# Pair products and their PSUM tiles: two column tiles become four tiles of 64 partitions

## The reference, cut to what matters

```python
e = jnp.stack([tbl_0[ids[:, 0]], ..., tbl_25[ids[:, 25]]], axis=1)      # (512, 26, 32)
x1 = jnp.einsum('bik,bjk,hij->bhk', e, e, W1) + b1[None, :, None]       # W1 (128, 26, 26)
x2 = jnp.einsum('bik,bjk,hij->bhk', x1, e, W2) + b2[None, :, None]      # W2 (128, 128, 26)
z = jnp.sum(jnp.concatenate([x1, x2], axis=1), axis=-1)                 # (512, 256)
h = jnp.concatenate([z, dense_ctx], axis=1)                             # 256 + 16
h = jnp.maximum(h @ W_top1 + b_top1, 0.0)                               # 512
h = jnp.maximum(h @ W_top2 + b_top2, 0.0)                               # 256
y = h @ W_top3
```

## Time and profile before

| what | value |
|---|---|
| median of 3 runs (lowest to highest) | 164.78 us (164.68 to 164.88) |
| the profiled execution: its own time | 163.22 us |
| its span, from first to last instruction | 161.4 us |
| busy: PE / PE weight loads / DVE / ACT / POOL | 133.6 / 118.2 / 106.7 / 70.6 / 93.5 us |
| mean granted TensorE clock over the span | 0.968 |

### The profile page before, as it was taken

One profiled execution on the slowest core, in us unless ns is written; L12 is line 12 of the kernel. 1 busy time (PEld: TensorE's weight loads), 2 busy tenths in 40 slices (PEclk: granted clock), 3 DMA queues, 4 the chain that ended last, 5 costly groups with the idle time before them and its releaser, 6 DMA issues.

```text
span 161.4 us, 4180 instructions
## 1 busy us (share of the span) xinstructions
PE 133.6 (83%) x1670; PEld 118.2 (73%) x1670; DVE 106.7 (66%) x413; ACT 70.6 (44%) x189; POOL 93.5 (58%) x100
## 2 busy tenths in 40 slices
PE   6437999910299668998999999799999979999994
PEld 6324666700299557987887899698789968999993
DVE  7889568973999999999106998950699993000000
ACT  1121788943336764041553810255381025683042
POOL 3778777787778777777777777777774000000000
PEclk9999999996559999999999999999999999999999
DMA  6995331000000403001010421000043000032000
GB/s 131 387 304 167 128 113 21 14 8 14 16 15 16 73 15 80 13 12 16 13 19 12 82 72 25 13 12 16 15 81 73 10 0 0 4 60 63 13 0 1
DMA packets 8539, 8.59 MB, mean 53 GB/s; under 512 B 3128, under 2 KB 7650, under 8 KB 8340
## 3 DMA queue, kind: packets, MB, share of 16 engines
q1 hardware_dynamic: 2668, 4.70, 8.9%
q10 hardware_dynamic: 2908, 2.12, 5.9%
q0 software_dynamic: 2944, 1.51, 5.9%
HBM read 7.28 MB, written 1.04 MB: 52 GB/s over the span
## 4 chain that ended last, share of the span: by engine, by line
PE 60%; POOL 17%; issue 6%; DVE 6%; ACT 6%; DMA 3%; ACTq 0%; SPq 0%
POOL emb L321 17%; PE z2p L673 15%; PE ring L636 13%; PE z2p L678 7%; PE ring L642 5%; PE h2y L729 5%; PE ring L657 3%; DVE emb L482 3%; PE ring L666 2%; PE h1p L720 2%; ACT v_in L810 2%; DVE ctx_x L478 2%; PE h1p L721 2%; DMA idx<-in_ids 1%; DMA emb<-in_tbl,idx 1%
## 5 line engine op out<-in xcount | busy, mean ns | idle before, releaser
L321 POOL DMA_INDIRECT emb<-in_tbl,idx x92 | 92.6, 1007 | 29.4 <-issue 27.7
L636 PE MATMUL ring<-r,l 128*64 128x104 f32 x256 | 27.4, 268 | 10.3 <-DVE l L519 10.3
L636 PEld LDWEIGHTS ring<-r,l 128*64 128x64 f32 x256 | 25.2, 147 | 13.0 <-DVE l L519 10.7
L637 PE MATMUL ring<-r,l 128*64 128x104 f32 x256 | 27.4, 268 | 0.0
L637 PEld LDWEIGHTS ring<-r,l 128*64 128x64 f32 x256 | 25.2, 147 | 0.0
L673 PE MATMUL z2p<-t_in,v_in 128*128 128x128 f32 x208 | 24.5, 277 | 0.8 <-ACT v_in L810 0.8
L673 PEld LDWEIGHTS z2p<-t_in,v_in 128*128 128x128 f32 x208 | 23.6, 192 | 1.2 <-ACT v_in L810 1.0
L835 ACT COPY t_in<-ring 128x416 f32<-128x416 f32 x32 | 16.2, 507 | 17.4 <-PE ring L637 17.4
L605 PE MATMUL ring<-w1s,w2t 128*128 128x352 f32 x52 | 17.5, 502 | 3.7 <-DVE w1s L375 3.7
L605 PEld LDWEIGHTS ring<-w1s,w2t 128*128 128x128 f32 x52 | 10.8, 210 | 10.0 <-DVE w1s L375 3.8
L519 DVE TENSOR_TENSOR l<-sg_a,l 128x192 f32<-128x192 f32 (+5 forms) x72 | 15.9, 301 | 0.1
(11 more groups left out here) (138 smaller groups left out, 208.2 us busy)
## 6 DMA issues: line engine op xcount, KB each, us to landing
w2t<-in_L_rec_W SPq DMA_DIRECT2D x1, 1664.0 KB, 7.5
emb<-in_tbl,idx POOLq DMA_INDIRECT x92, 2.4
wt<-in_W_top SPq DMA_DIRECT2D x2, 512.0 KB, 8.6
octet<-in_octet_ids SPq DMA_DIRECT2D x1, 750.0 KB
gram_scratch<-t_in ACTq DMA_DIRECT2D x4, 169.0 KB
gram<-gram_scratch ACTq DMA_DIRECT2D x4, 126.0 KB
small_tbl<-in_tbl SPq DMA_DIRECT2D x4, 125.0 KB
w<-in_L_rec_W SPq DMA_DIRECT2D x1, 338.0 KB, 7.9
```

The lines of the kernel that those rows point to most:

```text
L321: pool.indirect_dma_start(out=emb[:, g, f * K:(f + 1) * K], out_offset=None, in_=a[f"tbl_{f}"][:, :], in_offset=bass.IndirectOffsetOnAxis( ...
L636: pe.matmul(ps[0:HALF, s], l[:, t, 0:HALF], fields, start=True, stop=True)
L637: last = pe.matmul(ps[HALF:P, s], l[:, t, HALF:P], fields, start=True, stop=True)
```

## The change

1. **Tiles of 64 partitions.** A matmul on the block diagonal `R` is cut into its upper and lower 64 rows. A tile t has four matmuls instead of two: two halves h of the rows by two column tiles. Each has 64 rows, 64 (inner) or 42 (across) columns of weights, and half as many moving columns as before, 52 or 26, since a half of the rows holds two of the four samples. The two halves write to two banks. A call of `t_block` makes two blocks (`T_AT` is every second n), with 8 tiles (inner) or 16 (across) to a pair of banks. The blocks stay 8 and 4, and so do the copies and their elements; the copies write their samples two by two.
2. **A ring of four banks.** `z2p` moves into the last quarter of the bank `h2y`, and its bank joins the ring. Layer 3 of the last group writes to `sg_b`. `look_up` of the next group stands after blocks 3 and 5.
3. **Gram transfers on SP.** The five DMAs of each group are issued by SP. SP no longer passes on the gathers: DVE waits for `gathered` itself.
4. **Dummy products.** After `look_up(1)`, PE makes 38 products of `ident` with itself (`WARM_T`) ahead of the first cubes.
5. **Order on DVE.** The two picks for group 1 move from behind `own_terms(1)` into and ahead of `build_b(0)`. In groups 1 and 2 the across products of the first half go behind the fill of R, and the inner cubes wait for two steps of `pairs` there instead of three (`A_WHOLE`).
6. **SBUF.** The inputs of `wt1c` are loaded into `t_in`, which saves two tiles.

```diff
-BLK = 4
-NB = NT // BLK
-XBLK = 8
-TB = NB + NT // XBLK
+BLK = 8
+ROWS = 64
+NB = 2 * (NT // BLK)
+XBLK = 16
+TB = NB + 2 * (NT // XBLK)
-OH_AT = (4, 6)
-WARM_CTX, WARM_VA = 9, 7
-RING = 3
+OH_AT = (3, 5)
+WARM_CTX, WARM_T = 9, 38
+RING = 4
+A_WHOLE = (0, 3)
+T_AT = tuple(range(0, TB, 2))
...
-        zp = [None, ctx.enter_context(nc.psum_tensor("z2p", [P, 512], F32))[:, 0:P]]
-        h2p, yp = [h2y[:, m, :] for m in range(M2)], h2y[0:1, M2, :]
+        h2p, yp, z2p = [h2y[:, m, :] for m in range(M2)], h2y[0:1, M2, :], h2y[:, M2 + 1, :]
...
             for g in range(G):
-                for c, (f0, f1) in enumerate(PARTS):
-                    sp.wait_ge(gathered[g][c], 16 * rows_of(g, f0, f1))
-                    sp.sem_inc(part_in, 1)
+                sp.wait_ge(t_out, TB * g + NB)
+                sp.dma_start(gram_dram[0:NH * NF, :].rearrange("(u v) b -> u v b", v=NF),
+                             t_in[SGL:SGL + NH, :, :]).then_inc(gram_a_stored, 16)
...
@@ take_part
-                dve.wait_ge(part_in, 3 * g + part + 1)
+                dve.wait_ge(gathered[g][part], 16 * rows_of(g, f0, f1))
@@ build_a
-                products(0, across).then_inc(pairs, 1)
+                if g in A_WHOLE:
+                    products(0, across).then_inc(pairs, 1)
@@ build_b
                 fill_r(g, 1)
+                if g == 0:
+                    pick(1, 1)
                 take_part(g, 2)
...
                 fill_r(g, 2)
+                if g not in A_WHOLE:
+                    products(0, across).then_inc(pairs, 1)
                 products(1, across).then_inc(pairs, 1)
@@ t_block
                 if n < NB:
+                    pe.wait_ge(*bank_free("t", TB * g + n + 1))
+                    banks = [ps, bank_of("t", TB * g + n + 1)]
                     for i in range(BLK):
-                        t = n * BLK + i
-                        fields = R[:, t, :, :].rearrange("p q f -> p (q f)")
-                        s = slice(i * 4 * NF, (i + 1) * 4 * NF)
-                        pe.matmul(ps[0:HALF, s], l[:, t, 0:HALF], fields, start=True, stop=True)
-                        last = pe.matmul(ps[HALF:P, s], l[:, t, HALF:P], fields, start=True, stop=True)
+                        t = n // 2 * BLK + i
+                        s = slice(i * 2 * NF, (i + 1) * 2 * NF)
+                        for h in range(2):
+                            r = slice(h * ROWS, (h + 1) * ROWS)
+                            fields = R[r, t, 2 * h:2 * h + 2, :].rearrange("p q f -> p (q f)")
+                            pe.matmul(banks[h][0:HALF, s], l[r, t, 0:HALF], fields, start=True, stop=True)
+                            last = pe.matmul(banks[h][HALF:P, s], l[r, t, HALF:P], fields, start=True, stop=True)
...
+            keep_warm(WARM_T, bank_of("t", 3), bank_free("t", 3))
-            for n in range(TB):
+            for n in T_AT:
                 t_block(0, n, True)
```

More of the change, by code:

```diff
@@ L467, in one_hot, with pick @@
                 dve.wait_ge(octet_step, 4)
-            def pick(g):
+            def pick(g, only=None):
                 for kind, n in picks(g):
                     k = n % 2
+                    if only not in (None, k):
+                        continue
                     dve.wait_ge(picked, n + 1)
@@ L565, in _ @@
             add_unmixed(0)
+            pick(1, 0)
             build_b(0)
@@ L570, in _ @@
             own_terms(1)
-            pick(1)
             for g in range(1, G):
@@ L578, in _, with keep_warm @@
         def _(pe):
-            def keep_warm(count):
+            def keep_warm(count, bank, free=None):
+                if free:
+                    pe.wait_ge(*free)
                 for _ in range(count):
-                    pe.matmul(h1p[:, 0, :], ident[:, :], ident[:, :], start=True, stop=True)
+                    pe.matmul(bank[:, 0:P], ident[:, :], ident[:, :], start=True, stop=True)
             def prepare(n):
@@ new lines, in t_block @@
+                    return
+                pe.wait_ge(*bank_free("t", TB * g + n + 1))
+                banks = [ps, bank_of("t", TB * g + n + 1)]
+                for i in range(XBLK):
+                    t = (n - NB) // 2 * XBLK + i
+                    s = slice(i * 2 * NH, (i + 1) * 2 * NH)
+                    for h in range(2):
+                        r, q = slice(h * ROWS, (h + 1) * ROWS), slice(2 * h, 2 * h + 2)
+                        pe.matmul(banks[h][0:NX, s], l[r, t, P:P + NX], R[r, t, q, NH:NF], start=True, stop=True)
+                        last = pe.matmul(banks[h][HALF:HALF + NX, s], l[r, t, P + NX:LW], R[r, t, q, 0:NH], start=True, stop=True)
+                        if i == XBLK - 1:
+                            last.then_inc(t_done, 1)
@@ L672, in inner @@
                     for j in range(j0, j1):
-                        last = pe.matmul(zp[1], v_in[:, j, :], t_in[:, j, :], start=(start and j == j0), stop=(stop and j == j1 - 1))
+                        last = pe.matmul(z2p, v_in[:, j, :], t_in[:, j, :], start=(start and j == j0), stop=(stop and j == j1 - 1))
                     return last
@@ L677, in across @@
                     for j in range(NH):
-                        last = pe.matmul(zp[1], v_ac[0:MC, j, :], t_ac[0:MC, j, :], start=(start and j == 0), stop=(stop and j == NH - 1))
+                        last = pe.matmul(z2p, v_ac[0:MC, j, :], t_ac[0:MC, j, :], start=(start and j == 0), stop=(stop and j == NH - 1))
                     return last
@@ L767, in _ @@
             layer2(G - 2, h2p)
-            for n in range(TB):
+            for n in T_AT:
                 t_block(G - 1, n, False)
-                if n == L3_AT:
+                if n + 1 == L3_AT:
                     layer3(G - 2, yp)
```

73 lines of the change are left out of this document (29 added, 44 removed).

## The result

The change makes the kernel slower: 183.91 us (182.47 to 186.01, 4 runs) against 164.75 (164.68 to 164.88, 4 runs) on the same chip, a ratio of 1.113 (95% interval 1.107 to 1.120). The forecast was 157.3. The profiled execution took 183.91 for a span of 182.1, 20.7 more than the span before. Two of the warnings that the prediction set out are there: the clock dips after 45 us, and PE is the last to arrive at group 3.

A forecast was written before the change was run, and what follows sets the result against it. PE was taken to bound the kernel, with POOL's gathers and DVE close behind. Group 3 starting 5.4 us earlier plus 2.1 in its cubes gave 7.5 off 164.78: 157.3 us, range 155.0 to 162.0.

The forecast's parts named there:

- Two of the warnings: Signs of a wrong forecast: a clock dip after 45 us; PE still the last to arrive ahead of group 3.
- the price of a pass over a whole stage: Cut cubes on PE: passes of 58 and 39 ns, 6.2 us a group instead of 8.6, down 2.4.
- Rival A: Four tiles not side by side, or PE's issue too slow: 11.5 to 12.5 us a group, 174.7 us; chance 0.12.
- Rival D: The clock falls elsewhere: one spell at 0.50 costs up to 5 us of PE's work, 162.3 us; chance 0.07.
- The dummies: PE's pause before group 0's cubes: 76 passes, 8.7 us from 33.0 to 41.7, hold the clock and cost nothing.
- Group 0: Cubes start at 43.85, sums at 55.8 instead of 59.22, 3.4 us off; group 1's cubes start at 75.7.
- The ring and the copies: ACT's copies bound a cube stage: sums start 2.1 us sooner in group 3, 2.6 in groups 1 and 2.
- The gathers: Group 2's second part lands at 95.1; gathers hold group 3's start to 129.7 instead of 135.12, 5.4 us off.
- rival C: The gathers still land late: group 3 starts at 131.1, time 158.7 us; chance 0.17.
- SP: SP issues the gram's DMAs at no cost; ACT's 1.67 us issue goes, part of group 0's 3.4 us.

The follow-up runs named there:

- mixed: picks_late with the inner cubes of groups 1 and 2 alone cut into four tiles; 159.02 us, ratio 0.976 to the kernel before.
- ring3: pairs_all with a ring of three banks instead of four; 162.95 us, ratio 0.997 to the kernel before.
- a_whole: pairs_all with the first half's across products ahead of the second part in all four groups, as before the change; 159.84 us, ratio 0.981.
- gram_act: pairs_all with the gram's DMAs back on ACT's queue; 159.79 us, ratio 0.977 to the kernel before.
- across_split: pairs_all with each across matmul issued as two with half the moving columns, still 128 rows; 171.22 us, ratio 1.058 to the kernel before.
- pairs_all: The changed kernel without the cut, both kinds of cubes in pairs of 128 rows; 159.07 us, ratio 0.982 to the kernel before.
- no_dummies: pairs_all without the 38 dummy products; 160.51 us, 1.4 more than pairs_all.
- inner_quads: pairs_all with only the inner cubes cut into four tiles; 159.45 us, ratio 0.979 to the kernel before.
- picks_late: pairs_all with group 1's two picks behind the matrices of the second half, and 42 dummies; 158.84 us, ratio 0.981 to the kernel before.

## Why the prediction was wrong, and where it was right

**The step that failed is the price of a pass over a whole stage**: "With 2 ns between passes, as now, I take 58 and 39 ns: 64 x (58 + 39) = 6.2 us a group, down 2.4." Both lengths are right (59 and 41). But a group's cubes are now 1,024 instructions, and these would have to come at 6.1 ns each; over a stage they come at 13.1 [group 3 after: 13.50 us for 1,033]. The rows ahead of the prediction held no row on supply. A row of the page before had it:

```profile
q8 instruction: 13, 0.21, 0.5%
```

These are 13 pieces for 3,340 instructions of PE. Group 3's cubes ran at 522 instructions in 9.51 us, 18.2 ns each, with holes small enough to be taken for nothing. The 4 instructions in 45 ns that I read as a rate were a burst out of what had already been fetched.

The Trainium skill ("Runtime: NRT & Kernel Launch", Instruction fetch mechanics) says that instructions are refilled in blocks of 16 KiB, 256 of them, and that the fetch is hidden because instructions are issued more slowly than they come in. The size of the block agrees with every run here, where the pieces are PE's instructions over 256 to within one. That it is hidden does not: with four tiles PE starts a matmul with its load every 10 to 15 ns, a block is used up in 1.3 to 1.9 us, and the next one takes 3.4 to 4.2.

**Rival A** had the right size for half a reason. It named two ways to a longer pass, tiles that take turns, or PE's instructions "issued no faster than" a rate. The first is shown false: four tiles start within 20 ns. The second is what happened, but as blocks and not as a rate between neighbouring matmuls, and so it bears on the stage and not on the pass. Its formula, 121.2 + 4C, with C = 13.0 (15.70 less 2.7 for look-ups and layer 3) gives a span of 173.2; of the other 8.9 of the 182.1 the rests' clock takes 8.6. The chance of 0.12 was far too low, and the point from which it decides, C = 10.1, was right in kind: 13.0 lies well beyond it. The Trainium skill's 25 ns between starts ("TensorE: Matmul & The Clock Gate", Back-to-back issue gap), weighed there, does not hold across tiles here: starts are 10.2 ns apart. That it would have given a stage of nearly the measured length is a coincidence.

**Rival D**, the clock, was priced for a single spell caused by PE's waits for DVE, with the evidence of small holes that had left the clock at 1.00. What brought it down were the across cubes in four tiles, surely in groups 1 to 3 (a fall near 60 us comes in mixed, ring3 and a_whole as well, whose across cubes are not cut), and once, as it seems, the pause behind the dummies (the same fall comes in gram_act and a_whole, where no cube is cut); why these across cubes did it and not those of across_split, which have holes too, stays open. It came on top of A, which the cases, kept apart as they were, did not allow for: their sum, 8 to 9 us over A's 173, is the result.

**The dummies**: 8.65 us were measured for 76 passes, from 32.97 to 41.62, where 8.7 was forecast. They hold the clock through the pause; after them it fell at 45.0, 0.35 us into the cut cubes, but in pairs_all it did not fall there. By no_dummies they are worth 1.4 to 1.9 us. **Group 0** was forecast to start at 43.85 and to reach the sums at 55.8; without the cut it did at 44.22 and 56.94, and group 1 at 76.42 for 75.7. The 0.4 comes from POOL's calls; the stage itself took 0.8 longer than worked out, which was not followed further.

**The ring and the copies**: with passes of pairs, pairs_all is 0.8 us ahead of the kernel before in groups 1 and 2 and nothing in group 3; the forecast of 2.1 and 2.6 rested on the shorter passes. In inner_quads group 1's cubes took 10.66 where both cuts were forecast to give 10.1.

**The gathers**: the end of a fill of `R` follows the part by 7.0 us as read from the earlier trace rows, and group 2's part lands earlier, at 96.02 in inner_quads against 98.09 before, but not at 95.1. The start of group 3 was forecast to be bound by it at 129.7. In pairs_all and inner_quads it came at 130.82 and 130.26, each exactly one period of PE after group 2 (27.20 and 26.85): PE was still the last, with the gathers close behind (in inner_quads the part is taken at 122.87 and `R` is full at 129.86). So rival C never came to decide. **SP** as issuer costs and brings nothing, as forecast for the path, though the 1.67 us issue on ACT is gone and was put down as a part of group 0's 3.4.

A version without the cut of the cubes comes to about 159 us, or to 161.8 by the ratio of pairs_all to the 164.75 of the kernel before; both lie inside the forecast's range. This does not confirm the forecast: group 0's part of it holds roughly, but no pass is shorter there. The best versions (picks_late 158.84, mixed, pairs_all and inner_quads within 1 us of it) are about 2% faster than the kernel before beside them, and no interval puts the gain at over 3.4%.

## What to carry to other kernels

Before a product is cut into more and smaller matmuls, count the instructions of the stage, loads included and twice over for float32 as in these profiles, and hold them against the code that comes in: here 256 of PE's instructions for each 3.4 us. Cut only where a pass is long by its moving columns (89 to 59 ns), not where the load of the weights is already as long (45 to 41 ns), and only as far as look-ups or other long work around it spread the instructions. Idle time of PE put down to "issue", in holes a fixed number of instructions apart, is the sign in a profile, and the count of pieces on the instruction queue confirms it; a clock that falls behind such a stage is paid for in the next one.

## What the hardware showed that was not expected

Four tiles of 64 rows do load and run side by side: matmuls start 10.2 ns apart with 42 weight columns and 14.8 with 64, which is a load of 41 or 59 ns shared by four. With two row tiles of 84 weight columns and 26 moving ones, however, matmuls came 38 ns apart at full clock and 70 ns apart at half, and the clock was at 0.50 for 25.2 of the 30.9 us of the stretch, though PE had no hole. A block of 256 instructions came every 3.4 to 4.2 us at best, in a program with no other transfer at all as well as beside the gathers, so the other DMAs are not what limits it; the next transfer began only about 1.1 us after PE had gone on with the last. Small matmuls in tiles can bring the clock to half though PE is busy for most of the time, and the spells, up to 10.2 us in the network, reach into the stage behind the one in which they began.
